# First step of an attention and expert kernel: x first in its queue, Q in front of K, V's bias a step behind, rows of ones written at once

## The chip, the core and the metric

The kernel runs on one core of one Trainium2 chip, as one program of 20,970 instructions. The metric is the device time of one execution in microseconds (us); lower is better. Five engines work side by side and meet only at semaphores: PE (TensorE, matrix products), ACT (ScalarE), DVE (VectorE), POOL (GpSimd) and SP (SyncE, which here only issues transfers). ACT and POOL issue transfers too.

## The reference, cut to what matters

The input x has 32 batches of 112 rows of 256 numbers, ctx has 32 batches of 375 rows of 256. 16 heads of 16 columns each.

```python
Q = split_heads(layernorm(x) @ Wq + bq)
K = split_heads(ctx @ Wk + bk)
V = split_heads(ctx @ Wv + bv)
attn = softmax(Q K^T / sqrt(16))
x = x + tanh(g_xattn) * ((attn V) @ Wo + bo)
# then a layernorm, a router over 8 experts, the best 2 of them for each row:
x = x + tanh(g_ffn) * experts(layernorm(x))
```

## The kernel before, in words

All tiles are float32 in SBUF. The attention half runs as one loop of steps, `for i in range(FIRST, LAST + 1)` with `FIRST = -3`; every engine has its own copy of that loop and a function `step(i)` in it with twelve places, k = 0 to 11. A step is a pipeline stage: it works on batch a = i + 3 (normalize x, project Q and K), s = i + 2 (project V in three chunks), c = i + 1 (the row maxima of the scores), b = i (exponentials and the product with V) and e = i - 1 (output projection). So in step -3 only batch 0 is there, as a, and the start of the program is the time in which the stages come in one after another. After the loop the experts follow. The order of the work on each engine is written out by hand; nothing moves it.

The path of batch 0 at the start, with the lines of the kernel before:

- Loads. SP issues ctx of batch 0 (L189), Wk (L199), Wq (L200), bk (L201), bq (L202), Wv (L203) and two more ctx. ACT issues the two gates (L426, L427) and then x of batches 0 to 3 (`load_x(0)`, L417).
- Layernorm. DVE waits for x, does statistics (L662, L665) and half of the variance (L576); ACT takes a root by Ln and Exp (L435, L437); DVE polishes it and writes the normalized `xn` (L678).
- PE in step -3: the K projection's first half (`key_proj(a, 0)`, L871, k = 2), the transposes of xn (L941, k = 3), Q (L967, k = 5), the K projection's second half (L871, k = 8).
- ACT copies each result out of PSUM: xn_t (L489), K with its bias (L495), q_raw (L502). DVE writes K's low part (L696, semaphore `s_klo`). GpSimd masks Q (L347, L348, L351, semaphore `s_qlo`).
- When both parts of K and Q are in the tile `split`, 16 transfers lay them out as `stack` in slot 0: SP issues half of them (L227 to L230), ACT the other half (`stack_first`, L530 to L533).
- The row maxima are products of `stack` (PE, L860) that DVE reduces (L705); their negatives are transposed (L876), copied (L521) and laid into `stack` by GpSimd's transfers (L306), and then come the exponentials (L837).

V has no bias added. What bv would add is the same for every row, so bv @ Wo is folded into the output's bias: DVE scales bo (`bo_gated`, L745), spreads bv (`bv_col`) over the tile `o_t` (L748, semaphore `s_bvb`), PE multiplies it by Wo (L1033, at the end of step -2), and DVE adds it (L752, `s_bog`). In step -3 DVE does L745 and L748; it then waits for `bv_col`, which ACT loads with Wo by eight transfers (`load_out_weights`, L421, L423) behind its step -3 and ahead of `stack_first`.

Two tiles hold fixed ones: row 96 of `stack` in each of its three slots (GpSimd, L358, one memset of 1 x 3008 at the end of each of the steps -3, -2 and -1), and columns 16 to 31 of `v_sb` (L361, L362, end of step -2).

## Time and profile before

| what | us |
|---|---|
| median of 3 runs | 941.22 (940.12 to 943.02) |
| the profiled execution | 943.71 |
| its span, first to last instruction | 941.8 |
| PE busy in it | 863.2 (92%) |
| ACT, DVE, GpSimd busy | 418.2, 492.6, 474.9 |
| mean granted TensorE clock | 0.963 |

The profiled execution lies 2.5 us above the median. Of its 943.71 us, 1.9 lie outside the span. Times within the span count from its start. [...]

### The profile page before, as it was taken

How to read it: one execution, taken by the hardware profiler on the slowest of the kernel's cores; microseconds unless marked ns; L12 is line 12 of the kernel's file. 1: busy time of each engine (PE TensorE's matmuls, PEld its weight loads, DVE VectorE, ACT ScalarE, POOL GpSimd, SP SyncE). 2: the span in 40 equal slices, each digit the busy share in tenths (PEclk: the TensorE clock that was granted, in tenths of full speed). 3: DMA queues.
4: the chain of work that ended last, by engine and by line, in shares of the span. 5: the costliest groups of instructions: out<-in, count | busy, mean ns of one | idle time of the engine just before them, and what ended most of it. 6: DMA issues, size and time to landing. Idle time of an engine off the chain costs nothing.

```text
span 941.8 us, 20970 instructions
## 1 busy us (share of the span) xinstructions
PE 863.2 (92%) x7152; PEld 683.1 (73%) x7152; DVE 492.6 (52%) x1155; ACT 418.2 (44%) x1083; POOL 474.9 (50%) x565
## 2 busy tenths in 40 slices
PE   4689999999999999999999999860899999999995
PEld 2468888888888888788878887640577777777774
DVE  2465666866866766775785865735122222222221
ACT  2245556555655655565565565530222222222221
POOL 2353443454554455455455445353466565656653
PEclk9889999999999999999999999965899999999998
DMA  5656666666676665566566565018244344344332
GB/s 141 144 142 152 165 163 152 163 165 167 159 166 171 161 140 151 125 156 160 131 135 144 128 146 130 24 31 180 56 62 64 58 67 68 60 65 63 63 62 28
DMA packets 99246, 110.87 MB, mean 118 GB/s; under 512 B 28668, under 2 KB 80628, under 8 KB 99144
## 3 DMA queue, kind: packets, MB, share of 16 engines
q1 hardware_dynamic: 78296, 90.49, 41.1%
q0 software_dynamic: 18240, 16.83, 11.4%
q10 hardware_dynamic: 2608, 2.23, 1.0%
q8 instruction: 60, 0.98, 0.5%
q14 instruction: 42, 0.34, 0.1%
HBM read 34.11 MB, written 16.15 MB: 53 GB/s over the span
## 4 chain that ended last, share of the span: by engine, by line
PE 83%; DMA 8%; DVE 3%; issue 3%; POOL 1%; ACT 1%; ACTq 0%; POOLq 0%; SPq 0%; DVEq 0%
PE ps L1060 16%; PE ps L860 11%; PE ps L837 9%; PE ps L851 9%; PE ps L866 9%; PE ps L1095 8%; PE ps L871 8%; DMA stack<-negmax_t 4%; PE ps L1006 3%; PE ps L967 2%; PE ps L1077 2%; DVE negmax L705 2%; PE ps L1083 2%; DMA out_dram<-y,idx 1%; PE ps L959 1%
## 5 line engine op out<-in xcount | busy, mean ns | idle before, releaser
L705 DVE TENSOR_REDUCE negmax<-ps 112x2 f32<-112x750 f32 x256 | 240.7, 940 | 161.5 <-PE ps L860 160.3
L469 ACT ACTIVATE probs<-ps 125x448 f32<-125x448 f32 x384 | 208.9, 544 | 233.7 <-PE ps L837 233.7
L837 PE MATMUL ps<-stack 97*125 97x224 f32 x768 | 192.9, 334 | 5.7 <-DMA stack<-negmax_t 5.7
L306 POOL DMA_DIRECT2D stack<-negmax_t x128 | 69.4, 544 | 234.4 <-ACT negmax_t L521 226.6
L837 PEld LDWEIGHTS ps<-stack 97*125 97x125 f32 x768 | 130.9, 190 | 31.1 <-DMA stack<-negmax_t 7.1
L860 PE MATMUL ps<-stack 96*112 96x376 f32 x512 | 143.2, 361 | 8.5 <-DVE negmax L705 8.1
L404 POOL DMA_INDIRECT out_dram<-y,idx x63 | 100.2, 1590 | 97.0 <-issue 56.2
L816 DVE TENSOR_TENSOR h<-silu,ps 128x352 f32<-128x352 f32 x63 | 32.8, 521 | 170.3 <-PE ps L1060 170.3
L556 ACT ACTIVATE silu<-ps 128x352 f32<-128x352 f32 x63 | 29.2, 464 | 192.1 <-PE ps L1060 192.1
L871 PE MATMUL ps<-ctx_t,wk_sb 128*128 128x375 f32 x256 | 96.4, 500 | 10.3 <-DMA bk_sb<-in_L_xattn_bk_dram 9.7
L851 PE MATMUL ps<-probs,v_sb 125*32 125x112 f32 x3072 | 101.1, 265 | 0.3 <-ACT probs L469 0.3
L866 PE MATMUL ps<-wv_sb,ctx_t 128*125 128x256 f32 x384 | 100.7, 384 | 0.2 <-DVE bo_gated L752 0.2
L312 POOL DMA_INDIRECT slot_table<-pay,slots_i x64 | 64.7, 1011 | 70.2 <-PE ps L851 58.5
L860 PEld LDWEIGHTS ps<-stack 96*112 96x112 f32 x512 | 71.6, 177 | 33.2 <-issue 17.9
L1095 PE MATMUL ps<-w_sb,h_t 128*128 x378 | 92.1, 379 | 0.7 <-ACT h_t L560 0.7
L1095 PEld LDWEIGHTS ps<-w_sb,h_t 128*128 128x128 f32 x378 | 71.9, 190 | 20.5 <-issue 0.9
L1060 PE MATMUL ps<-w_sb,xg_t 128*128 x252 | 86.2, 464 | 0.6 <-ACT xg_t L564 0.6
L851 PEld LDWEIGHTS ps<-probs,v_sb 125*32 125x32 f32 x3072 | 69.9, 110 | 15.0 <-ACT probs L469 0.4
L395 POOL DMA_INDIRECT xg<-xn_scratch,idx x63 | 61.8, 981 | 30.1 <-issue 18.6
L866 PEld LDWEIGHTS ps<-wv_sb,ctx_t 128*125 128x125 f32 x384 | 69.4, 190 | 7.5 <-issue 0.6
L871 PEld LDWEIGHTS ps<-ctx_t,wk_sb 128*128 128x128 f32 x256 | 45.8, 199 | 28.1 <-issue 11.9
L1060 PEld LDWEIGHTS ps<-w_sb,xg_t 128*128 128x128 f32 x252 | 47.9, 191 | 18.4 <-issue 1.5
(163 smaller groups left out, 1193.1 us busy)
## 6 DMA issues: line engine op xcount, KB each, us to landing
stack<-split SPq DMA_DIRECT2D x252, 150.0 KB
ctx_t<-in_ctx_dram SPq DMA_DIRECT2D x32, 375.0 KB, 4.5
stack<-split SPq DMA_DIRECT2D x126, 94.0 KB
stack<-split SPq DMA_DIRECT2D x126, 56.0 KB
out_dram<-xa SPq DMA_DIRECT2D x32, 112.0 KB, 3.9
xn_scratch<-xn SPq DMA_DIRECT2D x32, 112.0 KB, 3.8
w_sb<-in_L_ffn_w_dram SPq DMA_DIRECT2D x8, 352.0 KB, 4.0
xa<-in_x_dram SPq DMA_DIRECT2D x6, 448.0 KB, 4.8
```

The lines of the kernel that those rows point to most:

```text
L306: gp.dma_start(dst[:, :, SKP + SQ * h:SKP + SQ * h + SQ], negmax_t[4 * h:4 * h + 4, half, :].bitcast(f32)).then_inc(s_nmrow[half][c % NSLO ...
L312: gp.indirect_dma_start(table, bass.IndirectOffsetOnAxis(ap=slots_i[:, u % 2, GB * k + j:GB * k + j + 1], axis=0), pay[:, UNITS[u][j], k, ...
L404: gp.indirect_dma_start(out, bass.IndirectOffsetOnAxis(ap=idx[:, t % NI, 0:1], axis=0), y[:, t % NY, :], None, compute_op=ALU.add).then_in ...
L469: act.activation(probs[:, g % 2, ch, :], ps[0:KW, EXPB + k % 2, 0:4 * SQ], ACT.Exp).then_inc(s_exp, 1)
L705: dve.tensor_reduce(negmax[:, half, :, p4], ps[0:SQ, MAXB:MAXB + 2, 0:SK], axis=AX.X, op=ALU.max, negate=True).then_inc(s_max, 1)
L837: last = pe.matmul(ps[0:KW, EXPB + k % 2, QW * m:QW * m + QW], stack[:, b % NSLOT, p, KW * ch:KW * ch + KW], stack[:, b % NSLOT, p, SKP:KQ ...
L851: last = pe.matmul(ps[32 * j:32 * j + 32, PVB, SQ * g:SQ * g + SQ], v_sb[:, b % NSLOT, ch, head, :], probs[:, g % 2, ch, SQ * j:SQ * j + S ...
L860: last = pe.matmul(ps[0:SQ, MAXB + h, 0:SKP], stack[0:ONE_ROW, c % NSLOT, t, SKP + SQ * h:SKP + SQ * h + SQ], stack[0:ONE_ROW, c % NSLOT, ...
L866: last = pe.matmul(ps[0:KW, bank, 0:EMB], ctx_t[:, s % NSLOT, n, KW * ch:KW * ch + KW], wv_sb[:, n, :], start=(n == 0), stop=(n == DC - 1))
L871: last = pe.matmul(ps[:, bank, 0:SK], wk_sb[:, n, P * m:P * m + P], ctx_t[:, a % NSLOT, n, :], start=(n == 0), stop=(n == DC - 1))
L1060: last = pe.matmul(ps[:, bank, 0:F], xg_t[:, t % NS, k, :], w[k][:, bass.ds(e, 1), :].rearrange("p e f -> p (e f)"), start=(k == 0), stop= ...
L1095: last = pe.matmul(ps[:, YB, 0:EMB], h_t[0:n, c, :], w2_sb[0:n, c, bass.ds(e_o, 1), :].rearrange("p e d -> p (e d)"), start=(c == 0), stop ...
```

## The change

x's first load goes from ACT's queue to the head of SP's, Wq follows it, and then come ctx and Wk. In step -3, PE does the transposes of xn and Q ahead of K's first half. ACT issues half of `load_out_weights` as soon as x has landed, ahead of its first root, and the other half with bo and the router's weights behind q_raw, so that none stands ahead of `stack_first`. ACT copies K's first half out behind q_raw. DVE's L745 and L748 move from the end of step -3 to the end of step -2, right ahead of L752. GpSimd writes all three rows of ones and v_sb's columns at its start.

```diff
 # SP
+            load_x(0)
+            sp.dma_start(wq_sb[:, :, :], ...).then_inc(s_wq, 16)
             load_ctx(0)
             sp.dma_start(wk_sb[:, :, :], ...).then_inc(s_wk, 16)
-            sp.dma_start(wq_sb[:, :, :], ...).then_inc(s_wq, 16)
+            sp.dma_start(bq_sb[:, :], ...).then_inc(s_wq, 16)
             sp.dma_start(bk_sb[:, :], ...).then_inc(s_wk, 16)
-            sp.dma_start(bq_sb[:, :], ...).then_inc(s_wq, 16)
 # GpSimd
             last.then_inc(s_split0, 1)
+            gp.wait_ge(s_split0, 1)
+            for n in range(NSLOT):
+                gp.memset(stack[ONE_ROW:ONE_ROW + 1, n, :, 0:SKP].bitcast(f32), 1.0).then_inc(s_one, 1)
+            gp.wait_ge(s_one, NSLOT)
+            gp.memset(v_sb[:, :, :, :, HD:HD + 1], 1.0)
+            gp.memset(v_sb[:, :, :, :, HD + 1:32], 0.0).then_inc(s_vpad, 1)
+            gp.wait_ge(s_vpad, 1)
             gp.wait_ge(s_msk, 1)
...
-                if -3 <= i < 0:
-                    gp.wait_ge(s_qlo, i + 4)
-                    gp.memset(stack[ONE_ROW:ONE_ROW + 1, i + 3, :, 0:SKP].bitcast(f32), 1.0).then_inc(s_one, 1)
-                    gp.wait_ge(s_one, i + 4)
-                if i == -2:
-                    gp.memset(v_sb[:, :, :, :, HD:HD + 1], 1.0)
-                    gp.memset(v_sb[:, :, :, :, HD + 1:32], 0.0).then_inc(s_vpad, 1)
 # ACT
-            load_x(0)
             act.wait_ge(s_gate, 32)
...
+            act.wait_ge(s_x[0], 16)
+            load_out_weights(0)
             root1(0)
             load_x(1)
-            act.dma_start(bo_sb[:, :], ...).then_inc(s_bo, 16)
-            act.dma_start(wr_sb[:, :], w_router).then_inc(s_wr, 16)
...
-                    if k in (4, 9) and a is not None:
+                    if k in ((7, 9) if i == FIRST else (4, 9)) and a is not None:
...
                         last.then_inc(s_q_raw, 1)
+                        if i == FIRST:
+                            load_out_weights(1)
+                            act.dma_start(bo_sb[:, :], ...).then_inc(s_bo, 16)
+                            act.dma_start(wr_sb[:, :], w_router).then_inc(s_wr, 16)
...
                 if i == -3:
-                    load_out_weights(0)
-                    load_out_weights(1)
                     stack_first((2, 3))
 # DVE: L745 to L748
-                if i == -3:
+                if i == -2:
                     dve.wait_ge(s_tanh, 1)
...
-                if i == -2:
                     dve.wait_ge(s_bo_ps, 1)
 # PE
-                    if k == (3 if i == FIRST else 1) and (a is not None or b is not None):
+                    if k == 1 and (a is not None or b is not None):
...
-                    if k == 2 and a is not None:
+                    if k == (6 if i == FIRST else 2) and a is not None:
```

GpSimd's queue at the start of the program, before. The first row is the last of its preparations; q_raw and q_mask are Q of batch 0 and the mask of the heads.

```order
L296 MEMSET split 128x4 x2
L347 TENSOR_TENSOR q_msk<-q_raw,q_mask 128x2x112 [waits s_q_raw,s_msk]
L348 TENSOR_TENSOR split<-q_raw,q_mask 128x2x112
L347 TENSOR_TENSOR q_msk<-q_raw,q_mask 128x2x112
L348 TENSOR_TENSOR split<-q_raw,q_mask 128x2x112
L351 TENSOR_TENSOR split<-q_msk,split 128x2x224 [waits s_qhi]
L358 MEMSET stack 1x8x376 [waits s_qlo]
```

The same place after the change:

```order
L297 MEMSET split 128x4 x2
L301 MEMSET stack 1x8x376 [waits s_split0]
L301 MEMSET stack 1x8x376 x2
L303 MEMSET v_sb 125x144 [waits s_one]
L304 MEMSET v_sb 125x144x15
L355 TENSOR_TENSOR q_msk<-q_raw,q_mask 128x2x112 [waits s_q_raw,s_msk,s_vpad]
L356 TENSOR_TENSOR split<-q_raw,q_mask 128x2x112
```

The memset of `stack` that stood behind the five operations on Q stands ahead of them, three times, and v_sb's two memsets behind it.

PE's queue from its first product to V's first chunk, before (xn is the normalized x, ctx_t the context):

```order
L871 MATMUL ps<-ctx_t,wk_sb 128x375 [waits s_ctx0,s_wk,s_ident]
L871 MATMUL ps<-ctx_t,wk_sb 128x375
L941 MATMUL ps<-ident,xn 128x112 [waits s_xn]
L941 MATMUL ps<-ident,xn 128x112
L967 MATMUL ps<-xn_t,wq_sb 128x112 [waits s_xn_t,s_wq]
L967 MATMUL ps<-xn_t,wq_sb 128x112 x3
L871 MATMUL ps<-ctx_t,wk_sb 128x375 [waits s_q_raw]
L871 MATMUL ps<-ctx_t,wk_sb 128x375
L866 MATMUL ps<-wv_sb,ctx_t 125x256 [waits s_wv]
```

The same place after the change:

```order
L942 MATMUL ps<-ident,xn 128x112 [waits s_xn,s_ident]
L942 MATMUL ps<-ident,xn 128x112
L968 MATMUL ps<-xn_t,wq_sb 128x112 [waits s_xn_t,s_wq]
L968 MATMUL ps<-xn_t,wq_sb 128x112 x3
L872 MATMUL ps<-ctx_t,wk_sb 128x375 [waits s_ctx0,s_wk]
L872 MATMUL ps<-ctx_t,wk_sb 128x375
L872 MATMUL ps<-ctx_t,wk_sb 128x375 [waits s_q_raw]
L872 MATMUL ps<-ctx_t,wk_sb 128x375
L867 MATMUL ps<-wv_sb,ctx_t 125x256 [waits s_wv]
```

K's first half (ctx_t, wk_sb 128x375) stood ahead of the transposes and of Q, and now stands between Q and K's second half.

ACT's queue from the copy of xn_t in step -3 onwards, before:

```order
L489 ACTIVATE xn_t<-ps 128x224 [waits s_xn_ps]
L495 ACTIVATE split<-ps,bk_sb 128x375 [waits s_k_ps]
L502 ACTIVATE q_raw<-ps,bq_sb 128x112 [waits s_q_ps]
L502 ACTIVATE q_raw<-ps,bq_sb 128x112
L495 ACTIVATE split<-ps,bk_sb 128x375 [waits s_k_ps]
L421 DMA wo_sb<-in_L_xattn_Wo_dram 32x2x256
L423 DMA bv_col<-in_L_xattn_bv_dram 32x2x1
```

Six more loads of wo_sb and bv_col follow there, and then `stack_first`. The same place after the change, down to the first of `stack_first`'s eight transfers:

```order
L489 ACTIVATE xn_t<-ps 128x224 [waits s_xn_ps]
L502 ACTIVATE q_raw<-ps,bq_sb 128x112 [waits s_q_ps]
L502 ACTIVATE q_raw<-ps,bq_sb 128x112
L422 DMA wo_sb<-in_L_xattn_Wo_dram 32x2x256
L424 DMA bv_col<-in_L_xattn_bv_dram 32x2x1
L422 DMA wo_sb<-in_L_xattn_Wo_dram 32x2x256
L424 DMA bv_col<-in_L_xattn_bv_dram 32x2x1
L506 DMA bo_sb<-in_L_xattn_bo_dram 112x256
L507 DMA wr_sb<-in_L_ffn_w_router_dram 8x256
L495 ACTIVATE split<-ps,bk_sb 128x375 [waits s_k_ps] x2
L534 DMA stack<-split 32x2x376 [waits s_qlo,s_klo,s_split0]
```

Four of the eight loads now stand ahead of this place, the other four and bo and the router's weights between q_raw and K's first copy.

## Rows read from the trace of the kernel before

**Rows 1.** Stretches: from:to, length, busy of PE, PEld, DVE, ACT, POOL, PEclk, DMA, GB/s.

```profile
25.00:26.00 1.00, 0.00 (x0) 0.00 (x0) 0.00 (x0) 0.00 (x0) 0.00 (x0) 0.64 0.91 211
...
32.00:33.00 1.00, 1.00 (x6) 0.73 (x5) 0.86 (x4) 0.60 (x2) 0.00 (x0) 0.94 0.00 0
...
52.00:53.00 1.00, 0.41 (x2) 0.00 (x1) 1.00 (x2) 0.00 (x0) 1.00 (x1) 0.80 0.27 62
65.00:75.00 10.00, 9.89 (x117) 8.08 (x116) 5.54 (x8) 5.50 (x13) 6.66 (x10) 1.00 0.22 50
```

**Rows 2.** The chain of waits at the start, in order of time: start us, us, what.

```profile
1.79 7.60 DMA xa<-in_x_dram
...
14.18 2.04 PE ps L967 x8
...
16.89 2.88 PE ps L871 x4
...
23.27 3.27 DMA bv_col<-in_L_xattn_bv_dram
...
30.70 1.61 PE ps L967 x8
...
35.62 1.06 PE ps L1033 x4
...
37.19 2.03 DVE xn L678
...
47.33 5.89 DMA stack<-negmax_t
```

**Rows 3.** Timeline, first 3 us: start us, us, engine, line, operation.

```profile
0.83 0.46 SPq L189 DMA_DIRECT2D ctx_t<-in_ctx_dram  x1
...
1.92 0.14 POOL L296 MEMSET split<- 128x4 f32 x2
2.01 0.16 DVE L658 TENSOR_REDUCE q_mask<-head_rows 128x2 f32<-128x8 f32 x1 [2.01 <-POOL head_rows L293]
2.20 0.17 DVE L659 TENSOR_SCALAR q_mask<-q_mask 128x2 f32<-128x2 f32 x1
```

**Rows 4.** The tile xa up to 60 us: duration ns min/median/max; its loads' landing.

```profile
L678 DVE TENSOR_SCALAR xn<-xa,mv,rstd x4: 407/1004/2115, 12.5 to 52.4; 112x256 f32<-112x256 f32 x4
...
DMA to landing us min/median/max: 4.2/5.7/7.6
```

**Rows 5.** Timeline, DVE's TENSOR_SCALAR beside GpSimd in step -1.

```profile
36.47 2.60 POOL L358 MEMSET stack<- 1x3008 f32 x1
...
37.10 2.12 DVE L678 TENSOR_SCALAR xn<-xa,mv,rstd 112x256 f32<-112x256 f32 x1
```

**Rows 6.** Timeline around 481 us, DVE's TENSOR_SCALAR beside GpSimd's queue.

```profile
480.75 2.42 DVE L576 TENSOR_SCALAR half<-mv 112x4 f32<-112x4 f32 x1
...
481.03 0.57 POOL L347 TENSOR_TENSOR q_msk<-q_raw,q_mask 128x224 f32<-128x224 f32 x1
...
482.59 0.55 POOL L348 TENSOR_TENSOR split<-q_raw,q_mask 128x224 fp32r<-128x224 f32 x1
```

**Rows 7.** Timeline, steps -3 and -2: the first root, ACT's transfers, the copy of xn_t.

```profile
11.26 0.17 DVE L576 TENSOR_SCALAR half<-mv 112x4 f32<-112x4 f32 x1
...
24.00 0.73 ACTq L530 DMA_DIRECT2D stack<-split  x1
...
28.87 0.62 ACTq L533 DMA_DIRECT2D stack<-split  x1
...
29.81 0.35 ACT L489 ACTIVATE xn_t<-ps 128x224 f32<-128x224 f32 x1
```

**Rows 8.** Timeline, steps -2 and -1: K's second half, its low part, the first maximum.

```profile
33.03 1.51 PE L871 MATMUL ps<-ctx_t,wk_sb 128*128 128x375 f32 x4
...
35.18 0.61 DVE L696 SCALAR_TENSOR_TENSOR split<-ps,bk_sb,split 128x375 fp32r<-128x375 f32 x1 [2.28 <-ACT split L495]
...
39.14 0.92 DVE L705 TENSOR_REDUCE negmax<-ps 112x2 f32<-112x750 f32 x1
```

More of the change, by code:

```diff
@@ L196, in load_x @@
                 sp.dma_start(xa[:, GB * g % NX:GB * g % NX + GB, :], x[GB * g:GB * g + GB, :, :].rearrange("b q d -> q b d")).then_inc(s_x[g % 4], 16)
+            load_x(0)
+            sp.dma_start(wq_sb[:, :, :], Wq.rearrange("(k p) n -> p k n", p=P)).then_inc(s_wq, 16)
             load_ctx(0)
             sp.dma_start(wk_sb[:, :, :], Wk.rearrange("(k p) n -> p k n", p=P)).then_inc(s_wk, 16)
-            sp.dma_start(wq_sb[:, :, :], Wq.rearrange("(k p) n -> p k n", p=P)).then_inc(s_wq, 16)
+            sp.dma_start(bq_sb[:, :], bq.rearrange("(k p) -> p k", p=P), allow_slow_non_contiguous=True).then_inc(s_wq, 16)
             sp.dma_start(bk_sb[:, :], bk.rearrange("(k p) -> p k", p=P), allow_slow_non_contiguous=True).then_inc(s_wk, 16)
-            sp.dma_start(bq_sb[:, :], bq.rearrange("(k p) -> p k", p=P), allow_slow_non_contiguous=True).then_inc(s_wq, 16)
             sp.dma_start(wv_sb[:, :, :], Wv.rearrange("(k p) n -> p k n", p=P)).then_inc(s_wv, 16)
@@ L453, in value_out @@
                 act.activation(v_sb[:, s % NSLOT, ch, :, 0:HD], ps[0:KW, bank, 0:EMB].rearrange("p (h d) -> p h d", d=HD), ACT.Copy).then_inc(s_v, 1)
+            act.wait_ge(s_x[0], 16)
+            load_out_weights(0)
             root1(0)
             load_x(1)
-            act.dma_start(bo_sb[:, :], bo.rearrange("(a b) -> a b", a=1).broadcast_to([SQ, EMB])).then_inc(s_bo, 16)
-            act.dma_start(wr_sb[:, :], w_router).then_inc(s_wr, 16)
             def step(i):
@@ L503, in step @@
                         last.then_inc(s_q_raw, 1)
+                        if i == FIRST:
+                            load_out_weights(1)
+                            act.dma_start(bo_sb[:, :], bo.rearrange("(a b) -> a b", a=1).broadcast_to([SQ, EMB])).then_inc(s_bo, 16)
+                            act.dma_start(wr_sb[:, :], w_router).then_inc(s_wr, 16)
                     if k == 7 and s is not None:
```

## Prediction, made before the changed kernel ran

> **What bounds the kernel now.** Read the stretches first. From 65 to 75 us PE is busy for 9.89 of 10 us at the full clock [rows 1], and the later stretches of the attention half look the same. So no edit can pay there, and this change edits only the first steps. What it gains at the start stays in the total one for one, because PE then runs the same instructions, full, from an earlier moment. The start has to be read from the chain of waits, in order of time. It goes: x lands at 9.39; DVE's statistics; Q on PE at 14.18; K's second half at 16.89 to 19.77; then ACT's weight loads, of which the last bv_col lands at 26.54; only then does DVE go on to xn of batch 1, and Q of batch 1 starts at 30.70; the product for the bias at 35.62; then xn of batch 2 for 2.03 us at 37.19; the maxima; and last the transfer of the negatives into stack, 5.89 us, until 53.2 [rows 2]. The change touches nearly every piece of this but the last. The timeline shows what each piece hides, so I go through it in that order.
>
> **Which clock.** K's second half in step -3 takes 2.88 us for four products [rows 2], in step -2 it takes 1.51 [rows 8]. [...] The record falls to 0.50 after PE has had nothing since about 21.5, and comes back at 32.1 [rows 1], 4.6 us after PE took up steady work at 27.5. [...]
>
> **Part 1: x first, and GpSimd's memsets.** x would land at 0.83 + 4.2 = 5.0 (first in SP's queue [rows 3]; 4.2 us is the shorter of the landings of x [rows 4]) to 5.5, against 9.39. That would be worth 4 us if DVE could use it. I think it can't. DVE's TENSOR_SCALAR on xn takes 0.41 us alone [rows 4], but 2.12 beside the memset of stack: it ends at 39.22, 0.15 us after the memset does at 39.07 [rows 5]. The four-element TENSOR_SCALAR of the half variance takes 0.17 us alone [rows 7] and 2.42 beside four GpSimd operations in a row, until 483.17, when the last of them ends at 483.14 [rows 6]. So size does not save it, and it does not get in between two GpSimd operations that stand back to back.
>
> After the change GpSimd writes three memsets of 2.60 us [rows 5] back to back. Its memset of split ends at 2.06, so with a hop they run from 2.1 to 9.8. DVE's TENSOR_SCALAR on q_mask comes at 2.20 [rows 3], 0.1 us too late, with everything on DVE behind it: statistics, x or no x. It gets in at 9.8 to 9.95. From there to the half variance it took 2.05 us before (9.39 to 11.43 [rows 2, 7]), which makes 12.0. v_sb's memsets are 144 + 2160 elements against 3008, by the same speed 2.1 us, and hold it until 12.0 as well, so 12.1 against 11.43: **0.7 us later than now**, although x is there 4 us sooner. ACT's four weight issues ahead of the root, at most 0.62 each [rows 7], are over by then and cost nothing; were DVE not held, they would end at about 8.5 and stand ahead of a root at 7.2. [...]
>
> **Part 2: Q ahead of K.** Q starts at 14.18 + 0.7 = 14.9 and takes 2.04, to 16.9. Now K's first half, 2.88 at this clock, comes between it and K's second half; before it was done while x was awaited. The clock comes back at 14.9 + 4.6 = 19.5, about where the first half ends (19.8), and the second takes 1.5: it ends at 21.3 against 19.77. [...] ACT's six issues behind q_raw (17.5 to 21.2 at 0.62) stand ahead of the copy of K's first half and end with it; they cost nothing beside K. From the end of K's second half to its low part it is 1.25 us (34.54 to 35.79 [rows 8]), so both parts of batch 0 are ready at 22.5.
>
> **Part 3: nothing ahead of stack_first, and no wait for bv.** Here the gain lies. stack_first starts at 22.5, not at 24.00 [rows 7], 1.5 earlier. DVE has no 3.27 us wait for bv_col [rows 2], and writes xn of batch 1 at 22.5. PE transposes it and does K's first half of batch 1 by 25. But Q of batch 1 needs ACT's copy of xn_t, and ACT is behind its eight issues: 29.49 and 30.16 before (28.87 + 0.62; 29.81 + 0.35 [rows 7]), so 28.7 now. What is late next is thus ACT's queue, not DVE. Q of batch 1 starts at 28.8 against 30.70 [rows 2]: **1.9 earlier**.
>
> PE has stood from 25 to 28.8, though, and I expect 0.50 again. Before, the return at 32.1 fell into this very place. Now Q takes 2.04, V's chunk 1.96 (2.88 x 256/375), to 32.8, and K's second half runs at half speed until 33.4 and ends at 34.6. Before it was 34.54 [rows 8]. **The 1.9 us are given back** to the clock: net 0.0.
>
> **Part 4: V's bias a step behind.** DVE's three operations now stand between K's low part and the product for the bias: at most 0.41 for bo_gated [rows 4] and, for 112 columns each, under that for the two of o_t, 0.5 together. With hops the product starts 1.3 later than at 35.6 [rows 2]. Queued behind it on PE is the first row maximum; GpSimd's sum onto x waits too, off the path. Against it, xn of batch 2 falls from 2.12 to 0.41, because the memset beside it is gone: 1.7 off. Net 0.4 earlier. GpSimd's last operations on Q could hold bo_gated for up to 0.4, so 0 to 0.4. The memset in step -1 that goes hid behind other waits: nothing. v_sb's memsets in step -2 were not awaited: nothing.
>
> **Sum.** Against the profiled execution, 943.71: Part 1 to 3 together 0.0, Part 4 -0.4, gives 943.3. That execution lies 2.5 above the median, so the forecast for the median is 941.2 - 0.4 = **940.8**.
>
> **Rivals.**
>
> A. *PE keeps the full clock* over the gap from 25 to 28.8. It is shorter than the 6 us before the fall at 25.4, but the record also falls at 52.7, with PE busy 0.41 of that microsecond [rows 1]. Then Q, V and K take 1.0, 1.0 and 1.5, with q_raw between: K ends 2.3 earlier, 938.5.
>
> B. *DVE gets in ahead of or between the three memsets.* The distance at 2.1 us is only 0.1. Then q_mask and the statistics are done when the half variance comes, which still waits until 9.95; the root passes, and xn waits for v_sb's memsets until 12.1, against 12.95 before and 13.65 in the forecast. All is 1.5 earlier: 939.3.
>
> C. *Memsets at this place don't hold DVE*, or x's early landing is used in full. Half variance at 7.3, root behind ACT's issues at 8.5, xn done at 9.8, 3.9 before the forecast: 936.9. Against it: rows 5.
>
> [...]
>
> **Chances.** Forecast 0.40, A 0.17, B 0.19, C 0.11, D 0.13. About 0.3% (2.8 us, so 938.4 and 944.0) is what a measurement of this kernel can tell from no change. Faster than that are C, half of A and a little of B: 0.22. Slower is the far end of D: 0.07. The rest, 0.71, is within. The range runs from 937.2, short of most of C, to 943.5, the centre of D.
>
> **What would show it.** L661 on DVE takes 7 to 8 us and ends just behind the third memset; x lands by 5.5 and the statistics start near 10 (B: at 5.5; C: half variance near 7.3). K's two halves run from 17 to about 21.3. The first transfer of stack_first leaves at 22.5, Q of batch 1 starts near 28.8 with the record at 0.50 (A: 1.00), the first L707 at 38.7 to 39.1, and the first exponential's product stays near 53. I am wrong if statistics start with x's landing, or if Q of batch 1 starts before 27.

## Result and the profile after

The changed kernel takes 937.01 us (median of 22 executions, 932.34 to 941.85) against 940.37 for the kernel before on the same chip (22 executions, 936.86 to 944.3): the ratio is 0.9964, with a 95% interval of 0.995 to 0.9977. It is 3.4 us faster, by the interval 2.2 to 4.7, where I had forecast 0.4. On a second chip (run h2 below) the ratio was 0.9951 [0.9928, 0.9973]. The profiled execution took 941.85 us, 4.8 above the median, with a span of 939.9; so the spans of the two profiles differ by only 1.9, and what the change does has to be read from its first microseconds and not from the spans. All executions of whole kernels are in the fast state; the medians of the cut kernels below take in slow ones too, and over the fast ones alone f3 lies 0.9 and not 2.5 above f2, g3 2.0 to 2.4 below the changed kernel and h3 6.3 below h4.

The start of the changed kernel, in the timeline (start us, length us, engine, line, operation; in brackets the idle time before it and what ended it):

```profile
0.83 0.40 SPq L196 DMA_DIRECT2D xa<-in_x_dram  x1
...
2.11 7.71 POOL L301 MEMSET stack<- 1x3008 f32 x3
2.20 2.53 DVE L661 TENSOR_SCALAR q_mask<-q_mask 128x2 f32<-128x2 f32 x1
...
6.52 1.41 DVE L664 BATCH_NORM_STATS2 st<-xa 112x6 f32<-112x256 f32 x4 [1.78 <-DMA xa<-in_x_dram]
7.40 0.20 ACT L430 ACTIVATE tanh_g<-gates_in 112x2 f32<-112x2 f32 x1 [4.30 <-DMA gates_in<-in_g_ffn_dram]
...
8.37 1.48 DVE L578 TENSOR_SCALAR half<-mv 112x4 f32<-112x4 f32 x1
...
10.07 1.95 POOL L304 MEMSET v_sb<- 125x2160 f32 x1
...
10.95 1.22 DVE L680 TENSOR_SCALAR xn<-xa,mv,rstd 112x256 f32<-112x256 f32 x1
```

The three memsets of stack run back to back, 2.11 to 9.82, as I had said. But the TENSOR_SCALAR on q_mask, which came 0.09 us behind the first of them, ends at 4.73, when that first one does (4.71), and not at 9.8. So DVE's queue is free when x lands at 6.50 (0.83 + 5.67), and the statistics start at 6.52. The next TENSOR_SCALAR, the half variance, comes at 8.37 in the middle of the third memset and is held to 9.85; xn is held by the large memset of v_sb to 12.17.

The chain of waits from there (start us, us, what), which answers to [rows 2]:

```profile
0.83 5.67 DMA xa<-in_x_dram
...
13.45 2.02 PE ps L968 x8
15.47 4.75 PE ps L872 x8
...
21.54 0.74 ACTq L534
...
27.22 0.36 ACT xn_t L489
...
27.63 2.05 PE ps L968 x8
29.68 1.73 PE ps L867 x4
31.40 2.35 PE ps L872 x4
...
35.80 1.13 PE ps L1034 x4
```

Gone from it are x's landing at 9.39 and the wait for bv_col. In their place stand ACT's eight issues from 21.54 to 26.90, and behind them ACT's copy of xn_t at 27.22, for which PE waits 4.04 us. Of the clock, stretches of one microsecond (columns as in [rows 1]; the clock is a share of full speed):

```profile
25.00:26.00 1.00, 0.00 (x0) 0.00 (x0) 0.00 (x0) 0.00 (x0) 0.00 (x0) 1.00 1.07 281
32.00:33.00 1.00, 1.00 (x3) 0.50 (x2) 0.00 (x0) 0.00 (x0) 0.92 (x2) 0.50 0.00 0
33.00:34.00 1.00, 1.00 (x4) 0.71 (x3) 0.00 (x0) 0.23 (x1) 0.70 (x1) 0.78 0.00 0
52.00:53.00 1.00, 1.00 (x5) 0.81 (x4) 0.62 (x1) 0.87 (x4) 0.00 (x0) 0.50 0.61 144
...
65.00:75.00 10.00, 9.89 (x118) 8.10 (x117) 6.13 (x10) 6.38 (x15) 5.25 (x7) 1.00 0.50 115
```

PE has nothing from 23.6 to 27.6; the clock's record falls to 0.50 within this gap, at 26.6, and is back at 33.4. It falls again at 50.5 and is back at 53.9. Before, the two falls lay at 25.3 to 32.1 and 52.6 to 59.4 [rows 1]. The place that answers to [rows 8] and [rows 5]:

```profile
34.90 0.35 DVE L747 TENSOR_SCALAR bo_gated<-bo_sb,tanh_g 112x256 f32<-112x256 f32 x1
...
35.28 0.47 DVE L750 TENSOR_SCALAR o_t<-head_rows,bv_col 128x112 f32<-128x112 f32 x2
...
35.80 1.12 PE L1034 MATMUL ps<-wo_sb,o_t 128*112 128x256 f32 x4 [0.99 <-DVE o_t L750]
...
37.36 0.40 DVE L680 TENSOR_SCALAR xn<-xa,mv,rstd 112x256 f32<-112x256 f32 x1
...
37.68 0.93 DVE L707 TENSOR_REDUCE negmax<-ps 112x2 f32<-112x750 f32 x1
```

bo_gated and the two of o_t take 0.35 and 0.47, xn of batch 2 takes 0.40, and the first row maximum starts at 37.68, against 39.14 [rows 8].

### The profile page after: what moved, and what is told of

Read it like the earlier page. It is cut to its first block, busy times and chain, and to the rows that moved or that the text cites. A ratio compares the mean times of both kernels' runs of the same rounds, so it can differ in the third digit from the quotient of the medians.

```text
span 939.9 us, 20971 instructions
## 1 busy us (share of the span) xinstructions
PE 863.7 (92%) x7152; PEld 684.9 (73%) x7152; DVE 492.5 (52%) x1155; ACT 417.8 (44%) x1083; POOL 474.5 (50%) x565
## 4 chain that ended last, share of the span: by engine, by line
PE 84%; DMA 6%; DVE 3%; issue 3%; POOL 1%; ACT 1%; ACTq 1%; POOLq 0%; SPq 0%; DVEq 0%
PE ps L1061 16%; PE ps L861 11%; PE ps L838 9%; PE ps L852 9%; PE ps L867 9%; PE ps L1096 8%; PE ps L872 8%; DMA stack<-negmax_t 3%; PE ps L1007 3%; PE ps L968 2%; PE ps L1078 2%; DVE negmax L707 2%; PE ps L1084 2%; DMA out_dram<-y,idx 1%; PE ps L960 1%
## 5 line engine op out<-in xcount | busy, mean ns | idle before, releaser
L838 PEld LDWEIGHTS ps<-stack 97*125 97x125 f32 x768 | 131.3, 190 | 29.5 <-DMA stack<-negmax_t 6.3
L817 DVE TENSOR_TENSOR h<-silu,ps 128x352 f32<-128x352 f32 x63 | 32.9, 521 | 172.1 <-PE ps L1061 169.6
```

Source lines behind the costliest of these rows:

```text
L838: last = pe.matmul(ps[0:KW, EXPB + k % 2, QW * m:QW * m + QW], stack[:, b % NSLOT, p, KW * ch:KW * ch + KW], stack[:, b % NSLOT, p, SKP:KQ ...
```

## Experiments

Four kernels ran whole, each beside the kernel before on one chip (its median there 941.87 us, 35 executions). A whole kernel scatters by 5 to 12 us from one execution to the next, as much as all that is in question or more, so the others, but for h1 and h2, were cut off behind step 3: they leave out the later steps, the rest of the router and the experts, last some 120 us and scatter by 1 to 5. For each the start of a few instructions was read as well. A part of the scatter is the clock: the mean granted clock of an execution tells how long it stood at 0.50, and for the cut kernels that is between 0.93 and 1.00, but for one execution of i1 (0.608).

### One part at a time, whole kernels

e1, V's bias alone: ACT's loads and DVE's three operations are moved, the rest is as before.

```diff
 # ACT, in the kernel before
+            act.wait_ge(s_x[0], 16)
+            load_out_weights(0)
             root1(0)
...
+                            load_out_weights(1)
...
-                    load_out_weights(0)
-                    load_out_weights(1)
                     stack_first((2, 3))
 # DVE
-                if i == -3:
+                if i == -2:
                     dve.wait_ge(s_tanh, 1)
```

> The kernel before with only this of the change: ACT's weight loads split and moved away from ahead of stack_first, and DVE's L745 and L748 a step later. Theory (the gain of the first steps is made by ACT's queue and by DVE no longer waiting for bv_col): stack_first leaves at about 21.2 us instead of 24.0, Q of batch 1 starts at 27 to 28 instead of 30.7, the first row maximum on DVE at 38.0 to 38.6 instead of 39.14, the time 1 to 2.5 us under the kernel before. Rival (x first is what pays): first row maximum at 39 or later, time within 0.5 us.

Measured: 944.06 us, ratio 1.0026 [1.0002, 1.0049]: slower by 2.2, if by anything. Q of batch 1 starts at 27.24, as early as in the changed kernel, but the first maximum only at 40.43, where I had expected 38.0 to 38.6. The timeline around the product for the bias shows why:

```profile
33.43 2.60 POOL L358 MEMSET stack<- 1x3008 f32 x1
...
34.24 1.94 DVE L747 TENSOR_SCALAR bo_gated<-bo_sb,tanh_g 112x256 f32<-112x256 f32 x1
...
36.09 0.37 POOL L361 MEMSET v_sb<- 125x144 f32 x1
36.22 2.17 DVE L750 TENSOR_SCALAR o_t<-head_rows,bv_col 128x112 f32<-128x112 f32 x2
...
36.32 1.94 POOL L362 MEMSET v_sb<- 125x2160 f32 x1
...
38.44 1.23 PE L1034 MATMUL ps<-wo_sb,o_t 128*112 128x256 f32 x4 [4.29 <-DVE o_t L750]
```

In step -2 GpSimd writes stack's row and v_sb's columns. bo_gated, moved into that step, ends at 36.18 with the one memset (36.03) and o_t at 38.39 with the last (38.26). PE waits 4.29 us for o_t. In the place where the bias stood before, bo_gated was held too (2.19 us), but behind it DVE waited for bv_col in any case.

The same lines hold something that matters below. The first of the two operations on o_t comes at 36.22, inside v_sb's first, short memset. That one ends at 36.46 and the second follows without a gap, and o_t does not get in between them: it takes 2.11 us and ends behind the second. It is the same in e4, f3 and f4 (2.11 each).

e2, x alone: `load_x(0)` goes from ACT's queue to the head of SP's.

```diff
 # SP, in the kernel before
+            load_x(0)
             load_ctx(0)
 # ACT
-            load_x(0)
```

> The kernel before with only x's first load at the head of SP's queue instead of ACT's. Theory: statistics start at 6 to 7 us, xn is written by 10, but PE's queue has K's first half ahead, which then waits for ctx, Wk and bk until 10 or later, and stack_first waits for ACT's weight loads: Q starts at 13 to 13.7 instead of 14.18, stack_first leaves at 23.2 to 23.8, the first row maximum comes 0 to 0.7 us earlier, the time 0 to 0.7 us under the kernel before. Rival (x first carries the gain): first row maximum 1.5 us or more earlier, time 2 us or more under.

Measured: 943.66 us, 1.002 [0.9998, 1.0041], no gain. The statistics start at 6.83 and xn at 10.08, but K's first half runs on PE from 9.69 to 12.53, so Q starts at 13.44, 0.7 earlier than before, and bv_col is waited for as ever. The first maximum comes 0.7 earlier, at 38.44.

e3, the rows of ones alone: GpSimd's memsets at its start, all else as before.

> The kernel before with only the rows of ones and v_sb's columns written at GpSimd's start. Theory (DVE gets in between memsets but not during one): the half variance, due at 11.26, is held to about 12.1 by v_sb's memset, Q starts 0.7 later; xn of batch 2 takes 0.41 instead of 2.12; first row maximum 0.5 to 1.2 earlier, time 0.5 to 1.2 us under the kernel before. Rival (what the profile after gained beyond the first maximum, 2 us, comes from the memset of step -1 that is gone): time 2 us or more under, with the first exponential's product 3 us earlier.

Measured: 941.67 us, 0.9997 [0.9973, 1.0022], the same. At the start it costs 0.6 (Q at 14.79, of which 0.2 is a later landing of x), in step -1 it gives back more: xn of batch 2 takes 0.41 instead of 2.12, and the first maximum starts at 37.84, 1.3 before that of the kernel before.

e4, the changed kernel with the memsets at their old places in GpSimd's steps.

> The changed kernel with the rows of ones and v_sb's columns back at their old places. Theory: nothing holds DVE at the start, half variance at about 8.5, root behind ACT's issues at 9.3, xn of batch 0 written at 10.5 to 10.9 (12.17 in the changed kernel), Q 1.4 earlier; given back where xn of batch 2 waits for a memset again, 1 to 1.7; first row maximum within 0.6 of the changed kernel's 37.68, time within 1 us of it. Rival (early ones carry the gain): time 2 us or more above the changed kernel.

Measured: 941.7 us, 1.0003 [0.9979, 1.0027]. Its half variance is not held (8.12) and the first maximum of this profile starts early, at 36.57, though o_t took 2.17 us and PE waited 4.08 for it. What follows from the four: no part alone, nor all without the early memsets, can be told from the kernel before as a gain. The scatter is too large to rank them. By the medians all four miss what I had expected: e1 was to gain 1 to 2.5 us, e2 up to 0.7, e3 0.5 to 1.2, and e4 was to be within 1 us of the changed kernel. For e1 and e4 the intervals exclude it; e4's does not touch the changed kernel's [0.995, 0.9977].

### The same, cut off behind step 3

f1 and f2 are the kernel before and the changed kernel, f3 is e4 and f4 is e1, each cut; the four ran on one chip.

> The kernel before, cut off after step 3: of the attention only batches 0 to 6 are begun, nothing of the router's later part and of the experts is computed. It is the measure for the three other cut kernels, since the 500 us of attention and 280 us of experts behind the first steps bring their own scatter. Theory: about 125 to 140 us, with less scatter than the whole kernel's (under 2 us between most runs).

> The changed kernel, cut off after step 3 in the same way. Theory (the whole gain of 3.4 us is made in steps -3 to 0): 2.5 to 4.5 us under the cut kernel before. Rival (part of the 3.4 us is made or lost later): under 2 us.

> The changed kernel with the ones at their old places, cut off after step 3. Theory (early ones keep bo_gated and o_t, moved to step -2, off GpSimd's memsets, but hold the first root; both cost about the same): within 1 us of the cut changed kernel. Rival (early ones carry the gain, as the whole kernels' times say): 2 us or more above it.

> The kernel before with only ACT's weight loads and DVE's two operations moved, cut off after step 3. Theory (what ACT's queue wins, 2 to 3 us, is lost where bo_gated and o_t stand behind two memsets, 4 us): 0.5 to 2.5 us above the cut kernel before. Rival: at or under it.

| kernel | median us (executions) | Q of batch 1 | first maximum | PE waits for o_t |
|---|---|---|---|---|
| f1, before | 125.35 (124.55 to 125.75) | 30.99 | 39.05 | none |
| f4, bias alone | 124.54 (123.85 to 126.09) | 27.75 | 40.87 | 4.04 |
| f3, late memsets | 123.55 (121.31 to 126.14) | 24.60 | 37.71 | 4.04 |
| f2, changed | 121.07 (120.25 to 121.91) | 26.77 | 36.34 | 0.99 |

The gain of 4.3 us stands out of the scatter here, and by the medians the memsets' place is worth 2.5 of it. The medians mix executions in which the clock fell for longer and for shorter. At a mean granted clock of 0.957 to 0.959 f1 has four (median 125.0), f3 two (122.94 and 124.15) and f2 two (121.33 and 121.91): so the gain is 3.4, and the memsets' place is worth about 1.9 of it, from few executions. By the executions compared it is 0.9 to 2.5, less than the 3.7 by which e4 and the changed kernel differ whole, each against the kernel before on its own chip. It isn't worth it at the start, where the early memsets cost time (f3 starts Q of batch 1 2.2 earlier), but in step -2, where the late ones hold bo_gated and o_t as in e1 (1.69 and 2.17 us). xn of batch 1 is held by a late memset too (1.96 us in f3, 0.40 in f2), but ACT's queue is later than that in both. What moving the bias is worth alone stays open: f4 is 0.8 under f1 in time, where I had expected 0.5 to 2.5 over, although its first maximum is 1.8 later (in the profile of its longest execution, 126.09), and e1 was 2.2 over the kernel before. f3 is a miss as well: I had expected it within 1 us of f2.

### The held TENSOR_SCALAR

g1 tests what my forecast said would happen at the start. It is the changed kernel, cut, with one memset over all three rows instead of three:

```diff
-            for n in range(NSLOT):
-                gp.memset(stack[ONE_ROW:ONE_ROW + 1, n, :, 0:SKP].bitcast(f32), 1.0).then_inc(s_one, 1)
+            gp.memset(stack[ONE_ROW:ONE_ROW + 1, :, :, 0:SKP].bitcast(f32), 1.0).then_inc(s_one, NSLOT)
```

> The changed kernel, cut off after step 3, with one memset over the three rows of ones instead of three memsets. The failed step of the prediction was that DVE doesn't get in between the three. Theory (DVE gets in where one memset ends and the next begins, so one long memset must do what was predicted): the TENSOR_SCALAR on q_mask takes 7 to 8 us, statistics start at 9.8 to 10, Q at 14.6 to 15, and the time is 1 to 2.5 us above the cut changed kernel's 121.07, 122.1 to 123.6. Rival (the early end of q_mask had another cause): statistics at 6.3 as in the changed kernel, 120.3 to 121.9.

Measured: 123.48 us (121.69 to 124.32), 1.7 to 2.4 over the changed kernel (which, cut, gave 121.07, 121.80 and 121.09 on three other chips; g1 to g4 ran together on a fourth, without it, and are held against these). At a clock of 0.957 or 0.958 the difference is 1.4 (median 123.72 of five executions against 122.3 of eight). The timeline of its start:

```profile
2.15 7.61 POOL L275 MEMSET stack<- 1x9024 f32 x1
2.17 7.61 DVE L579 TENSOR_SCALAR q_mask<-q_mask 128x2 f32<-128x2 f32 x1
...
6.82 3.38 DVE L582 BATCH_NORM_STATS2 st<-xa 112x6 f32<-112x256 f32 x4
...
10.65 1.34 DVE L496 TENSOR_SCALAR half<-mv 112x4 f32<-112x4 f32 x1
...
13.09 0.41 DVE L598 TENSOR_SCALAR xn<-xa,mv,rstd 112x256 f32<-112x256 f32 x1
```

The same elements, the same 7.6 us on GpSimd, and now q_mask's TENSOR_SCALAR takes 7.61 us and ends with the memset. The statistics of x are through at 10.2, not at 7.9; xn starts at 13.09, Q at 14.80 and the first maximum at 38.22. What I had forecast for three memsets is what one long one does. In GpSimd's work the only thing that differs is the boundaries, and at the first of them, at 4.7 us, DVE gets in. One thing is cheaper than forecast: the four statistics, whose records begin at 6.82, are through 0.4 us after the held operation (9.78), not 1.4, and the half variance comes 0.9 after it, not 2.05. That gained nothing, as v_sb's memset holds the half variance to 11.99.

g3 takes the third row and v_sb's columns out of the way: GpSimd writes two rows at its start and the rest behind the normalization of batch 1.

```diff
-            for n in range(NSLOT):
+            for n in range(2):
                 gp.memset(stack[ONE_ROW:ONE_ROW + 1, n, :, 0:SKP].bitcast(f32), 1.0).then_inc(s_one, 1)
+            gp.wait_ge(s_xn, 1)
+            gp.memset(stack[ONE_ROW:ONE_ROW + 1, 2, :, 0:SKP].bitcast(f32), 1.0).then_inc(s_one, 1)
             gp.wait_ge(s_one, NSLOT)
```

> The changed kernel, cut off after step 3, with two rows of ones written at GpSimd's start and the third and v_sb's columns only once xn of batch 0 is written. Theory (half variance and xn of batch 0 are held by GpSimd's memsets for 1.5 and 0.8 us): half variance at 8.2 in 0.17, xn of batch 0 written at 10.1 to 10.5 instead of 12.14, all that follows 1.5 earlier; time 0.8 to 2 us under 121.07. Rival (these holds are covered by ACT's queue or by K): within 0.5 us.

Measured: 120.25 us (118.42 to 121.4), 0.8 to 1.5 under the changed kernel. The half variance takes 0.17, xn starts at 9.90 and Q at 11.61 instead of 13.43. Of these 1.8 us 1.0 are left at Q of batch 1 (25.81) and 0.6 at the first maximum (35.75) against f2. Against i2, the profile of the changed kernel in which K takes as long as here (4.92 and 4.85 us), it is 1.7 and 1.9.

### ACT's eight issues and the clock

g4 lets SP issue three of the four groups of batch 0's transfers, and ACT one, so that ACT has four issues fewer ahead of xn_t of batch 1.

```diff
-                for g in range(2 if s == 0 else 4):
+                for g in range(3 if s == 0 else 4):
...
-                    stack_first((2, 3))
+                    stack_first((3,))
```

> The changed kernel, cut off after step 3, with SP issuing three quarters of batch 0's transfers into stack and ACT one quarter. Theory (in step -2 ACT's eight issues ahead of the copy of xn_t are the bound): the copy of xn_t of batch 1 2.5 us earlier, PE's gap 1.5 instead of 4 us, the full clock kept in at least some runs; time 1.5 to 4 us under 121.07. Rival (the transfers' landing becomes the bound for the first row maximum): first maximum not earlier, time within 1 us.

Measured: 118.19 us (117.3 to 118.41), 2.9 to 3.6 under the changed kernel. xn_t of batch 1 is copied at 23.73, Q of batch 1 starts at 24.14 and takes 1.15 instead of 2.05: PE has waited 1.34 us, and the clock has not fallen yet (it does at 31.8). The first maximum starts at 31.90. At a clock of 0.971 it is 2.5 under the changed kernel.

g2 leaves the issues and takes the clock's fall away: six idle products, of ctx_t and wk_sb into a bank that holds nothing, fill the gap ahead of Q of batch 1.

```diff
                         if a == 0:
                             pe.wait_ge(s_wq, 32)
+                        if a == 1:
+                            for _ in range(6):
+                                pe.matmul(ps[:, 1, 0:SK], wk_sb[:, 0, 0:P], ctx_t[:, 1, 0, :], start=True, stop=True)
```

> The changed kernel, cut off after step 3, with six more products (wk_sb by ctx of batch 1, written to a PSUM bank that nobody reads) on PE between K's first half and Q of batch 1, where PE stood still for 4 us. Theory (the gap costs the full clock, which Q, V and K of batch 1 then lack): Q of batch 1 at 1.0 instead of 2.05 us, K's second half of batch 1 ends 2 to 2.5 us earlier, the time 1 to 2.5 us under the cut changed kernel's 121.07. Rival (the clock falls anyway, or the second fall in step -1 takes the gain back): within 0.7 us of 121.07.

Measured: 118.77 us (117.91 to 120.38), 2.3 to 3.0 under the changed kernel, with more work in it. The stretches at the two falls, first of the changed kernel cut (f2), then of g2:

```profile
25.00:26.00 1.00, 0.00 (x0) 0.00 (x0) 0.00 (x0) 0.00 (x0) 0.00 (x0) 0.50 1.03 224
...
50.00:51.00 1.00, 1.00 (x6) 0.99 (x5) 0.00 (x0) 0.42 (x1) 0.00 (x0) 0.50 0.49 115
```

```profile
25.00:26.00 1.00, 1.00 (x5) 0.62 (x4) 0.00 (x0) 0.00 (x0) 0.00 (x0) 1.00 1.05 233
...
50.00:51.00 1.00, 1.00 (x8) 0.92 (x9) 0.48 (x1) 0.79 (x2) 0.00 (x0) 1.00 0.93 202
```

PE is busy in 25 to 26 and the record stays at 1.00, there and at 50 to 51. Q, V and K's second half of batch 1 run at full speed (1.15, 1.13 and 1.43 us). The clock's price at this place, which the prediction took as 2.3 (case A), is 2.3 to 3.0 with what the second fall costs.

### Both edits, and whether the head's gain is kept

h1 is the whole changed kernel with the edits of g3 and g4, h2 the changed kernel itself, h3 and h4 are the same two cut. The four ran on one chip, where the kernel before took 937.64 us.

> The full changed kernel with two edits together: GpSimd writes two of the three rows of ones at its start and the third, with v_sb's columns, behind the normalization of batch 1; and of the eight transfers that ACT issues ahead of its copy of xn_t of batch 1, SP issues four (three of four groups), so ACT has four fewer. In the kernels cut off behind step 3 the one edit took 0.8 us off and the other 2.9, against a changed kernel on another chip. If a gain of the head is kept to the end and the two add, this kernel is 3 to 4.5 us under h2 on this chip: near 0.9955 of it, and 0.992 of the kernel before. If the head's gains are eaten later, it is within 1.5 us of h2.

> The changed kernel unaltered, as the anchor on this chip: 0.9964 of the kernel before (0.995 to 0.998).

> The kernel of h1 cut off behind step 3; everything later is left out. First row maximum at 31 to 32.5, the first exponential's product near 46. 3 to 4.5 us under h4 if the two edits add; the same as the edit of the transfers alone (2.9) if SP's three groups already take all that can be had.

> The changed kernel cut off behind step 3, as the anchor on this chip for the cut kernels: 121.1 (120.2 to 122), the profiled one with the clock at 0.50 in two places. If chips differ by as much as the edits of g1 to g4 moved the time (0.8 to 2.9), it comes out under 120 or over 122.

| | whole | cut |
|---|---|---|
| changed | 934.47 (930.39 to 936.35) | 121.80 (120.21 to 122.87) |
| both edits | 929.90 (925.97 to 931.25) | 114.92 (114.52 to 117.40) |
| difference | -4.6 | -6.9 |

The whole kernel with both edits is at 0.9902 [0.9873, 0.993] of the kernel before, 7.7 us under it. Cut, the two edits give more than I expected (6.9 against 3 to 4.5) and more than the two apart (at most 1.5 + 3.6), and the first maximum comes at 30.34, ahead of the expected 31 to 32.5. A good part of it is the clock again: in four executions of h3 its mean is 1.00 (114.52 to 114.95), in the other two 0.97 (116.64 and 117.40), and these two lie 3.6 under the three of h4 at 0.971 or 0.972, as I had expected. In h1's head it falls once, from 29.5 to 32.9. The new start, in the timeline of h1:

```profile
8.08 0.17 DVE L580 TENSOR_SCALAR half<-mv 112x4 f32<-112x4 f32 x1
...
9.75 0.41 DVE L682 TENSOR_SCALAR xn<-xa,mv,rstd 112x256 f32<-112x256 f32 x1
...
21.62 0.35 ACT L491 ACTIVATE xn_t<-ps 128x224 f32<-128x224 f32 x1
...
22.02 1.15 PE L970 MATMUL ps<-xn_t,wq_sb 128*128 128x112 f32 x8 [1.38 <-ACT xn_t L491]
...
26.69 0.67 DVE L749 TENSOR_SCALAR bo_gated<-bo_sb,tanh_g 112x256 f32<-112x256 f32 x1
```

A gain at the head is kept for the most part: 4.6 of 6.9 in this pair, and in the pair before and changed 3.4 and 3.2 whole against 4.3 cut. In the profiles of h1 and h2 the end of step 0 stands 6.1 us apart and the end of the span 7.0. I can't say whether the whole kernel gives back a part of it or whether the medians of 6 and 9 executions that scatter by 5 merely miss it.

### The order of Q and K

i1 is the changed kernel, cut, with K's first half ahead of the transposes again and, on ACT, its copy ahead of q_raw; i2 is the changed kernel, cut, on the same chip.

```diff
 # PE
-                    if k == 1 and (a is not None or b is not None):
+                    if k == (3 if i == FIRST else 1) and (a is not None or b is not None):
...
-                    if k == (6 if i == FIRST else 2) and a is not None:
+                    if k == 2 and a is not None:
 # ACT
-                    if k in ((7, 9) if i == FIRST else (4, 9)) and a is not None:
+                    if k in (4, 9) and a is not None:
```

> The changed kernel with PE's and ACT's old order in the first step (K's first half ahead of the transposes and Q, its copy ahead of q_raw), cut off behind step 3; everything later is left out. In the profile of the kernel with only x moved, K's first half ran from 9.69 to 12.53, while x was being normalized, and Q started at 13.44, as in the changed kernel. If K's first half is free there, K's second half of batch 0 ends near 19.0 (16.1 + 2.9) and not at 19.0 to 20.2 behind Q, and this kernel is 0 to 1.3 us under the changed one: the new order of Q and K costs up to that. If Wk, which is fourth in its queue here and third there, comes later, K's first half ends behind 12.9 and pushes the transposes and Q back by as much: then this kernel is 0 to 1 slower.

> The changed kernel cut off behind step 3, as the anchor on this chip: 121.1 to 121.8, as on the two chips before. The start of Q of batch 1 moves with the moment at which the clock comes back in K of batch 0, which differed from one profile to the next (eight products of K in 3.8 to 4.9 us from the same start).

Measured: i1 120.45 us (119.54 to 121.89, and one execution of 162.81 with a mean granted clock of 0.608, whose cause is open), i2 121.09 (119.33 to 122.83). PE in the first step of i1:

```profile
9.48 2.84 PE L732 MATMUL ps<-ctx_t,wk_sb 128*128 128x375 f32 x4 [9.48 <-DMA bk_sb<-in_L_xattn_bk_dram]
...
13.37 2.02 PE L828 MATMUL ps<-xn_t,wq_sb 128*128 128x112 f32 x8 [0.54 <-ACT xn_t L429]
16.08 2.87 PE L732 MATMUL ps<-ctx_t,wk_sb 128*128 128x375 f32 x4 [0.69 <-ACT q_raw L442]
```

K's first half fits ahead of the transposes, Q starts at 13.37, no later than behind the new order (13.43), and K's second half ends at 18.95, where the changed kernel has it between 19.05 (h4) and 20.21. So the new order brings nothing; it may cost 0.6, which is within the scatter. It costs so little because in the new order the clock comes back within K's eight products, while here all four of the second half run at the half speed (2.87 us).

That return is also where a part of the scatter comes from. The eight products of K start at 15.24 to 15.27 in all five profiles of the changed kernel, whole or cut, but end differently. Of h4, the shortest:

```profile
15.25 3.80 PE L732 MATMUL ps<-ctx_t,wk_sb 128*128 128x375 f32 x8
```

| profile | K's eight products | Q of batch 1 | first maximum |
|---|---|---|---|
| h4 | 3.80 | 26.42 | 35.55 |
| f2 | 4.05 | 26.77 | 36.34 |
| h2 | 4.70 | 27.51 | 37.38 |
| i2 | 4.92 | 27.53 | 37.60 |
| first profile | 4.94 | 27.63 | 37.68 |

The later K ends, the later come the other two. K's end 1.1 us later goes with a first maximum 2.1 later: Q of batch 1 comes 1.2 later, and in h4 Q of batch 1 still runs at full speed (1.15 us) before the clock falls.

## Why the prediction was wrong

The time, 937.0, lies 0.2 outside my range of 937.2 to 943.5, and it is faster by more than 0.3%, for which I gave 0.22. Step by step:

**What bounds the kernel: right.** PE is full from step 0 on (9.89 of 10 us at 65 to 75 in both), and a gain at the head is largely kept at the end. That it stays one for one, as I wrote, is not shown (4.6 of 6.9).

**Part 1 failed, at one sentence:** "it does not get in between two GpSimd operations that stand back to back". I took it from [rows 6], where the half variance is held for 2.42 us beside four TENSOR_TENSORs. For the three memsets of stack it is false: L661 ended at 4.73, and g1 shows the boundary to be the cause, since without it the forecast came true (Q at 14.80, forecast 14.9). That was rival B's mechanism, at 0.19. At this place q_mask's operation took 2.53 us beside a first memset of 2.60. Not every boundary lets DVE in, though: in the changed kernel too, DVE's half variance outlasts four TENSOR_TENSORs of GpSimd.

```profile
476.28 0.50 POOL L314 DMA_DIRECT2D stack<-negmax_t  x1 [2.45 <-issue]
...
476.52 2.42 DVE L578 TENSOR_SCALAR half<-mv 112x4 f32<-112x4 f32 x1
...
476.80 0.57 POOL L355 TENSOR_TENSOR q_msk<-q_raw,q_mask 128x224 f32<-128x224 f32 x1
...
478.36 0.55 POOL L356 TENSOR_TENSOR split<-q_raw,q_mask 128x224 fp32r<-128x224 f32 x1
```

It was even there first, 0.28 us ahead of the first of the four, while GpSimd was still issuing a transfer. Nor do v_sb's two memsets let it in in e1: they hold o_t past the boundary between them (2.11 us). So [rows 6] were read rightly and carried over wrongly, to another operation, and which boundaries let DVE in is not settled by either reading: the first one between the memsets of stack does, the one between v_sb's two memsets and those between the TENSOR_TENSORs do not. With B's figures the rest of Part 1 is right to 0.1 us: half variance held to 9.85 (9.95), xn done at 12.17 (12.1). x landed in 5.67 us, not in 4.2 to 4.7 (Wq, ctx and the rest are issued right behind it; that they are the reason no run tests); a second error that cost nothing, as the third memset holds DVE longer. That ACT's four issues cost nothing was right, by a smaller margin than it seemed: the gates land at 7.40 and the issues end at 9.18, 0.7 ahead of the root.

**Part 2: right in its mechanism, too dear by itself.** K's two halves end at 20.2; shifted by B's 1.5 the forecast had 19.8. But the 1.5 us that it put on the new order (21.3 against 19.77) are too much: against i1 K's second half ends 0.1 to 1.3 later, the less the earlier the clock comes back, and in the medians it is 0.6, within the scatter.

**Part 3: right.** stack_first starts at 21.54 and Q of batch 1 at 27.63 (forecast 22.5 and 28.8; the 1.0 and 1.2 between are what is left of Part 1's 1.5). ACT's queue is what is late next, g4 confirms it. The clock fell, Q took 2.05, and most of the gain was given back: K's second half ends at 33.74, 0.8 before 34.54 [rows 8], with Q 3.1 earlier. The record was back 5.8 us behind the start of Q and not 4.6, and K's second half took 2.54 instead of 1.8. That every start after a gap costs the same 4.6 us no run shows: from the start of Q to the record's return it is 4.8 us in f2 and 5.4 in h2. Case A's mechanism (no fall up to K's end) was seen only where something was done for it (g2, g4, h1, h3); for Q alone also in h4, e4, f3 and f4. Half speed through nearly all of both first steps stands in the profile of e1: there K's first half of batch 1 takes 2.73, Q 2.05 and K's second half 2.26.

**Part 4: right in sum, for a reason it left out.** The product for the bias starts at 35.80, 2.1 behind K's end, where it had stood 1.1 behind it: 1.0 later, against 1.3 forecast. xn of batch 2 takes 0.40. I wrote that the late memsets in step -2 "were not awaited: nothing". That holds for the kernel before alone. With the bias moved there they would have been awaited: the product starts 2.6 us later in e1 (38.44 against 35.80), and f3 takes 0.9 to 2.5 us longer than f2, by the executions compared. The early memsets are what makes Part 4 cheap.

**The size: B's 1.9 was short.** At the first maximum of the first profiles it is 1.5 (37.68 against 39.14 [rows 8]; forecast 38.7 to 39.1). But that profile has the latest return of the clock of all: over the five of the changed kernel the first maximum starts at 36.91 in the mean, against 39.14 and 39.05 in the two of the kernel before (first profile and f1), so the gain there is 2.2. The first exponential's product, forecast near 53, starts at 50.76, 50.38, 49.91, 49.59 and 48.50, against 53.36 and 51.83: 2.8. Case B counted the moved instructions alone, with one moment for the clock; that moment is a term of its own, worth 2 us between its early and late ends. In the changed kernel it falls within K's eight products; before, K's second half ran through at half speed in both profiles (2.88 [rows 2] and 2.87). That the clock's moment makes up what B lacked is read from these profiles, and no run holds it fixed. The rest, from 2.8 to the median's 3.4, is within its interval [2.2, 4.7]. In the first pair of profiles the landing of the negatives (5.89 us before [rows 2], 4.7 at most after, to 60 us) and the second fall of the clock (6.8 us before, 3.4 after) raise the difference to 3.8 by the end of step 0 (82.48 against 86.33), and the chain of the changed kernel goes by PE and DVE there and no longer by that transfer; since f1 has a second fall of 3.4 too, and h2 none there, I count neither as the change's. Which part of such differences it causes stays open.

**The range** missed by 0.2. A hit by as little would have been luck, since the forecast it stood around had Part 1 wrong and B, the nearest rival, gave 939.3. It ended at 937.2 because I left out most of case C, and its inner bounds came from the moved work alone; nothing was set aside for the moment of the clock's return, which differs from one execution to the next. Its upper end, the centre of D, rests on a clock at half speed through both first steps. No run of the changed kernel shows that: in its five profiles K's eight products took 3.80 to 4.94 us, against 5.7 at half speed throughout (twice the 2.87 for four), and the longest of its 22 executions took 941.85 us.

## What to carry to other kernels

Work that GpSimd does only once belongs where DVE has nothing to do: a long memset holds a TENSOR_SCALAR of either size tried to its end (q_mask for 7.61 us beside one of 7.61 in g1, xn for 2.12 instead of 0.41 in the kernel before), and DVE's queue behind it. Three memsets of 2.6 us instead of one of 7.6 let DVE in (q_mask in 2.53 us), but short instructions are no rule: those of 0.37 and 0.55 us did not. Where a step is moved, look at what GpSimd runs beside it in its new place and not only in its old (o_t took 0.47 us for both operations with no memset beside it, 2.17 with v_sb's): three edits, none of which could be told from no gain by itself in the whole kernel, gained together with the new order of Q and K. And when PE waits in a head, its gap costs twice, once as a wait (4.04 us ahead of Q of batch 1 in the changed kernel) and once as half clock behind it (Q in 2.05 us instead of 1.15), so that filling the gap or halving the issues ahead of it (g2, g4: 2.3 to 3.6 us) was worth nearly as much as the whole change.

## What the runs showed of the hardware

- DVE's TENSOR_SCALAR gets in at the boundary between the first two memsets of stack on GpSimd (2.53 us beside three of 2.6) and is held to the end of a single one (7.61 of 7.61). It does not get in between v_sb's memsets of 0.37 and 1.94 us (2.11 us in e1, e4, f3 and f4), and it outlasts four TENSOR_TENSORs of GpSimd (2.42 us, in both kernels). Why these differ no run here tells.
- Two elements on each of 128 partitions (q_mask) are held to a memset's end like 256 on 112 (xn). Statistics (BATCH_NORM_STATS2) beside the memsets of stack are not held: 1.41 us for four, as without a memset before; queued behind a held TENSOR_SCALAR they are through 0.4 us after it (g1).
- K's products of 375 columns take 0.72 us each at the start (four in 2.87) and 0.36 (four in 1.44) from a moment on that differs by over 1 us between executions of one kernel, though K's products start at the same time to 0.03 us. Each fall that the records of the heads show is 3.4 or 6.8 us long (6.8 and 3.4 in the first profile of the changed kernel, twice 6.8 in that of the kernel before).
- In the first profile of the changed kernel x of 448 KB lands in 5.67 us at the head of the queue, with 1.9 MB issued behind it, and the gates, 0.4 KB each, land only at 7.40.
- In the changed kernel each issue of a transfer into stack costs ACT 0.61 to 0.74 us of its queue, those of its loads 0.32 to 0.58; eight of the first kind are 5.4 us, in which it computes nothing.
